# Three linked empty GpSimd instructions behind each of 512 indirect transfers

## The chip, the cores and the metric

The kernel runs on one core of one Trainium2 chip. The metric is the device time of one execution in microseconds (us); of the kernel before, the median of three runs is 880.05 us.

## The reference

An input x of 32 x 256 rows of 128 numbers (float32) goes through three layers that each add to it: half of a feed-forward layer with 16 experts, an attention-like layer with a complex running sum, and half of the same expert layer again. Cut to what matters:

```python
x = L0_attn_x
x = x + 0.5 * _L0_ffn_ref(_layernorm(x, axis=-1), ...)
x = x + _L0_attn_ref(_layernorm(x, axis=-1), ...)
x = x + 0.5 * _L0_ffn_ref(_layernorm(x, axis=-1), ...)

def _L0_ffn_ref(x, Wr, br, W1, b1, W2, b2):      # every row goes to its best two of 16 experts
    probs = softmax(xt @ Wr + br)
    w, idx = top_k(probs, 2)
    comb = zeros((T, E)).at[arange(T)[:, None], idx].add(w / sum(w))
    h = gelu(einsum('td,edh->teh', xt, W1) + b1)
    o = einsum('teh,eho->teo', h, W2) + b2
    return xt + einsum('teo,te->to', o, comb)

def _L0_attn_ref(x, gamma, wq, wk, wv, wa, wg, wo):
    q, k, v, a, g = xn @ wq, xn @ wk, xn @ wv, xn @ wa, xn @ wg
    # a becomes a complex factor of magnitude below one
    y_t = a_t * y_(t-1) + k_t * v_t               # an associative scan over the sequence
    return (q * real(y) * silu(g)) @ wo
```

## The kernel before

The 8192 rows are cut into four groups (g = 0 to 3) of 16 tiles of 128 rows. Each of the two expert layers (f = 0 and 1) handles a group as follows. The router (stages R and K) finds for each row its two experts and the place that it gets in a table sorted by expert, and leaves the places in `IDX`. GpSimd **scatters** (stage P) each tile twice, once for each chosen expert, into a table `rows_in` in the chip's memory: 32 indirect transfers for a group, the first 16 at L466 and the others at L474, with a small copy (L471) of the weights ahead of each eight of the latter. SyncE then loads `rows_in` in pieces into `xs` (L366) and the weights of the experts into `WUP` (L360). TensorE, with ScalarE, works through 24 **pairs** of tiles in a group (stage E, cut into sub-stages such as pairs 0 to 8, 8 to 20 and 20 to 24): it turns `xs` over (L776), multiplies with the first weights (L786) and, behind the gelu of ScalarE, with the second (L803). ScalarE moves each pair's result into `eo` (L540) and stores it into `rows_out`. GpSimd **gathers** (stage G) from there into `got` at L487, again 32 indirect transfers for a group, and VectorE adds `got` to `X` (stage C, L1069 and L1070). Between the layers a group goes through the attention stages (T, A0, A, I, H, A1, J, AP, U, A2, A3); its products on TensorE are at L863.

A table `ORDER` at the head of the file lists all stages; each engine walks it and takes its own part, so it sets the order on every engine. GpSimd's order is P00, P01, G00, P02, G01, P03, G02, P10, G03, P11, G10, P12, G11, P13, G12, G13 (the digits are f and g; G(0,3), G(1,1), G(0,2), P(1,3) and G(1,3) are issued in parts). There are 8 x 32 scatters and 8 x 32 gathers, 512 transfers.

GpSimd does not run ahead freely. Two tables, `PAIRS_BY` and `PRODUCTS_BY`, hold for each transfer how many pairs (semaphore `eo_sb`) and attention products (`proj_ps`) must be done before it is issued; `keep_behind` (L448) turns them into waits. A gather also waits for the stores of its group's pairs, a scatter for `IDX`. SyncE waits for the landed scatters of a group ahead of its first `xs` (L380, L381).

`link` (L419) lets an instruction raise a semaphore `pool_chain` at its end and makes the next instruction of GpSimd wait for it. 

Of the kernel before, what the change touches and what calls it, by code (L numbers as in the profile page):

```python
# [16 lines left out]
P = 128  # L17
# [3 lines left out]
G = 4  # L21
T = B * N // G // P
# [97 lines left out]

SLOT = {(f, g, 0): g for f in range(2) for g in range(G)}
SLOT.update({(f, g, 1): (g + 1) % G for f, g in HALVED})
# [3 lines left out]
def build(nc, x, gamma, wq, wk, wv, wa, wg, wo, wr, br, w1, b1, w2, b2, out):  # L126
# [43 lines left out]
    def rows_put(f, g, half):  # L170

        if half == 1:
            return XBUF + HALVED.index((f, g)), 16 * TILES[f, g, 1]
        rn = kind_no[("R", f, g)]
        return rn % XBUF, 16 * sum(TILES[st[1], st[2], 0] for st in kind_no if st[0] == "R"
                                       and kind_no[st] <= rn and kind_no[st] % XBUF == rn % XBUF)

    with ExitStack() as ctx:
# [236 lines left out]
        @block.gpsimd  # L415
        def _(pool):
            chain = [0]

            def link(ins):  # L419
                chain[0] += 1  # L420
                ins.then_inc(pool_chain, 1)
                pool.wait_ge(pool_chain, chain[0])

            pool.memset(zeros, 0.0).then_inc(zero_ready, 1)
            pool.memset(ones[:], 1.0)
            pool.memset(onesf[:], 1.0)
            link(pool.memset(ones_sq, 1.0))
            pool.affine_select(out=ident[:], in_=ones_sq, compare_op=ALU.is_equal, fill=0.0, base=0,
                               pattern=[[-1, P]], channel_multiplier=1)
            pool.affine_select(out=before[:], in_=ones_sq, compare_op=ALU.is_gt, fill=0.0, base=0,  # L430
                               pattern=[[1, P]], channel_multiplier=-1)
            link(pool.iota(iota_i, [[1, NT]], base=0, channel_multiplier=0))
            pool.tensor_scalar(centre[:], ident[:], 2.0, -2.0 / D, mult, add)
            link(pool.memset(keep[:], 1.0))
            pool.memset(keep[:, :, 0:1], 0.0)
            pool.memset(marks[:], 0.0)
            pool.tensor_copy(iota_f[:], iota_i).then_inc(consts, 1)
            pool.memset(B2[:], 0.0).then_inc(bias_clear, 1)

            pool.wait_ge(up_bias_in, 16)  # L440
            link(pool.tensor_copy(bias_parts[:, 0, :], raw_bias))
            link(pool.tensor_tensor(bias_rest, raw_bias, bias_parts[:, 0, :], sub))
            link(pool.tensor_copy(bias_parts[:, 1, :], bias_rest))
            pool.tensor_tensor(bias_parts[:, 2, :], bias_rest, bias_parts[:, 1, :], sub).then_inc(up_bias_split, 1)

            waited = [0, 0]

            def keep_behind(st, i):  # L448
                if i % 1 == 0 and PAIRS_BY[st][i // 1] > waited[0]:
                    waited[0] = PAIRS_BY[st][i // 1]  # L450
                    pool.wait_ge(eo_sb, waited[0])
                if i % 1 == 0 and PRODUCTS_BY[st][i // 1] > waited[1]:
                    waited[1] = PRODUCTS_BY[st][i // 1]
                    pool.wait_ge(proj_ps, waited[1])

            def scatter(n, m, f, g, half):
                slot, tiles = SLOT[f, g, half], TILES[f, g, half]
                b, (which, _) = kind_no[("R", f, g)] % XBUF, rows_put(f, g, half)
                first = T - tiles if half else 0
                parts = [range(first, first + tiles // 2), range(first + tiles // 2, first + tiles)]  # L460
                pool.wait_ge(rows_ready, n + 1)
                pool.wait_ge(zeroed[slot], 16 * ZEROS)
                for i, part in enumerate(parts):
                    for j in part:
                        keep_behind(("P", f, g, half), j - first)
                        pool.indirect_dma_start(rows_in[slot], bass.IndirectOffsetOnAxis(IDX[:, g, j, 0:1], 0),  # L466
                                                XL[:, b, j, :], None).then_inc(first_put[i], 16)
                for i, part in enumerate(parts):
                    pool.wait_ge(first_put[i], 8 * sum(TILES[st[1:]] for st in kind_no if st[0] == "P" and kind_no[st] <= m))
                    mine = slice(part[0], part[-1] + 1)  # L470
                    link(pool.tensor_copy(XL[:, b, mine, D:D + 1], WGT[:, g, 1, mine].unsqueeze(2)))  # L471
                    for j in part:
                        keep_behind(("P", f, g, half), tiles + j - first)
                        pool.indirect_dma_start(rows_in[slot], bass.IndirectOffsetOnAxis(IDX[:, g, j, 1:2], 0),  # L474
                                                XL[:, b, j, :], None).then_inc(scattered[which], 16)

            def gather(n, f, g, lo, hi):
                half = lo * T // 4 // TILES[f, g, 0]
                rows = (2 * TILES[f, g, half] + E - 1) * P
                for u in range(2):  # L480
                    pool.wait_ge(eo_out[u], 16 * (pairs_by[f, g, half] // SLOTS))
                for j in range(lo * T // 4, hi * T // 4):
                    if n > 0 and j % 4 == 0:
                        pool.wait_ge(combined, (n - 1) * 4 + j // 4 + 1)
                    for k in range(2):
                        keep_behind(("G", f, g, lo, hi), 2 * j - lo * T // 2 + k)
                        pool.indirect_dma_start(got[:, k, j, :], None, rows_out[SLOT[f, g, half]][0:rows, :],  # L487
                                                bass.IndirectOffsetOnAxis(IDX[:, g, j, k:k + 1], 0)).then_inc(got_in[j // 4], 16)

            for st in ORDER:  # L490
                if st[0] == "P":
                    scatter(kind_no[("K",) + st[1:]], kind_no[st], *st[1:])
                if st[0] == "G":
                    gather(gathers.index(st[1:3]), *st[1:])
# [696 lines left out]
```

## Time and profile before

| | |
|---|---|
| median of three runs | 880.05 us (880.0 to 881.23) |
| profiled execution, first to last instruction | 994.3 us |
| mean granted TensorE clock in it | 0.858 |
| TensorE busy in it | 725.1 us (73%) |
| VectorE, ScalarE busy | 546.3 us, 514.7 us |
| GpSimd busy | 590.6 us (59%), 551 instructions |
| indirect gathers, L487 | 256, mean 1117 ns |
| indirect scatters, L466 and L474 | 128 each, mean 1227 and 1065 ns |

The profiled execution's own time is known by its span alone, and that is 114.3 us longer than the median of the runs without a profile. So a time read from the profile is not simply a time of a timed run. In the page, a group's busy time is the number of instructions by their mean duration; the idle time behind it is that of its engine just before these instructions, by what ended it. "issue" means that nothing the profile shows was waited for.

### The profile page before, as it was taken

To read this page: it belongs to the slowest core of one execution; us is meant where nothing else is said; L and a number is where in the kernel's file an instruction comes from. 1 tells how busy PE (TensorE), PEld (TensorE's weight loads), DVE (VectorE), ACT (ScalarE), POOL (GpSimd) and SP (SyncE) were. 2 spreads that over 40 slices of the span, in tenths; PEclk is the share of its full clock that TensorE was granted. 3 is DMA by queue.
4 is the path that set the end of the run, shared out by engine and by line. 5 is a ranking of instruction groups with operands and counts; after the bars stand their busy time and mean duration, and the time that the engine had idled before them with its cause. 6 is when DMAs were issued, how large, how long until landed. Compare 5 with 4: busy or idle time off the path is not lost.

```text
span 994.3 us, 15862 instructions
## 1 busy us (share of the span) xinstructions
PE 725.1 (73%) x4409; PEld 607.2 (61%) x4410; DVE 546.3 (55%) x1352; ACT 514.7 (52%) x1071; POOL 590.6 (59%) x551
## 2 busy tenths in 40 slices
PE   4775888786876888669777967685968648977761
PEld 4234788685366873469644867534958627777650
DVE  7983103106689955799745996647876455010201
ACT  1111556455777637676277773576664315444340
POOL 2277441555777747758467457378657545655555
PEclk9995899889977989789788779795989759999986
DMA  9995587774146833176441456321758517778863
GB/s 327 299 348 165 149 234 228 208 202 130 40 123 195 224 111 105 42 202 194 121 124 46 129 161 202 99 66 40 217 167 250 141 41 199 221 207 226 234 201 103
DMA packets 188846, 167.13 MB, mean 168 GB/s; under 512 B 18976, under 2 KB 176480, under 8 KB 187744
## 3 DMA queue, kind: packets, MB, share of 16 engines
q1 hardware_dynamic: 120736, 106.83, 36.6%
q0 software_dynamic: 16384, 33.72, 11.5%
q10 hardware_dynamic: 51648, 25.63, 8.8%
q8 instruction: 39, 0.64, 0.3%
q14 instruction: 39, 0.32, 0.1%
HBM read 104.57 MB, written 61.51 MB: 167 GB/s over the span
## 4 chain that ended last, share of the span: by engine, by line
PE 48%; issue 12%; ACT 12%; another core or an unknown queue 9%; SPq 7%; DVE 5%; DMA 5%; ACTq 0%; DVEq 0%
PE bank L786 17%; PE bank L803 16%; PE bank L863 7%; DMA WUP<-up_weights 4%; PE bank L776 4%; ACT eo L540 2%; SPq L319 2%; PE bank L758 2%; SPq L360 1%; SPq L330 1%; ACT hidT L532 1%; PE bank L702 1%; ACT ci L623 1%; ACT xsT L551 1%
## 5 line engine op out<-in xcount | busy, mean ns | idle before, releaser
L487 POOL DMA_INDIRECT got<-rows_out,IDX x256 | 285.8, 1117 | 194.2 <-ACT eo L540 86.5
L786 PE MATMUL bank<-xsT,WUP 128*128 128x128 f32 x1564 | 240.0, 303 | 77.4 <-ACT xsT L551 51.1
L786 PEld LDWEIGHTS bank<-xsT,WUP 128*128 128x128 f32 x1564 | 218.8, 216 | 85.9 <-issue 75.2
L803 PE MATMUL bank<-W,hidT 128*128 x1564 | 221.0, 286 | 41.5 <-ACT hidT L532 32.1
L803 PEld LDWEIGHTS bank<-W,hidT 128*128 128x128 f32 x1564 | 199.3, 199 | 51.4 <-issue 49.6
L466 POOL DMA_INDIRECT rows_in<-XL,IDX x128 | 157.1, 1227 | 109.3 <-DVE IDX L1039 46.5
L474 POOL DMA_INDIRECT rows_in<-XL,IDX x128 | 136.3, 1065 | 91.7 <-ACT eo L540 53.7
L540 ACT ACTIVATE eo<-bank,xs 128x128 f32<-128x128 f32 x391 | 122.7, 367 | 109.9 <-PE bank L803 74.6
L532 ACT ACTIVATE hidT<-bank 128x512 f32<-128x512 f32 x200 | 118.1, 591 | 116.1 <-PE bank L786 72.8
L551 ACT ACTIVATE xsT<-bank 128x256 f32<-128x256 f32 x200 | 74.0, 377 | 86.2 <-remote 39.2
L863 PE MATMUL bank<-XT,WA 128*128 128x512 f32 x192 | 94.6, 654 | 21.2 <-DVE qg L1090 10.4
L776 PE MATMUL bank<-ident,xs 128*128 128x128 f32 x391 | 81.8, 301 | 5.7 <-issue 3.1
L1069 DVE TENSOR_TENSOR X<-got,X 128x512 f32<-128x512 f32 x32 | 22.0, 686 | 116.3 <-DMA got<-rows_out,IDX 102.2
L863 PEld LDWEIGHTS bank<-XT,WA 128*128 128x128 f32 x192 | 39.1, 207 | 72.8 <-issue 57.6
L1062 DVE TENSOR_TENSOR X<-bank,X 128x512 f32<-128x512 f32 x32 | 21.3, 687 | 96.5 <-issue 41.4
L776 PEld LDWEIGHTS bank<-ident,xs 128*128 128x128 f32 x391 | 56.4, 161 | 8.5 <-issue 8.2
L712 PE MATMUL bank<-WR,hidT 128*128 128x16 f32 x192 | 38.9, 341 | 21.9 <-issue 20.9
L712 PEld LDWEIGHTS bank<-WR,hidT 128*128 128x128 f32 x192 | 38.5, 297 | 23.9 <-issue 23.8
L758 PE MATMUL bank<-B,CT 128*128 128x512 f32 x64 | 37.0, 708 | 15.8 <-issue 9.0
L913 DVE BATCH_NORM_STATS2 stats<-X 128x6 f32<-128x128 f32 x192 | 38.3, 278 | 6.0 <-DMA X<-in_L_attn_x 5.8
L1011 DVE TENSOR_SCALAR den<-gexp 128x16 f32<-128x16 f32 x8 | 1.4, 173 | 62.0 <-ACT gexp L516 60.8
L969 DVE TENSOR_SCALAR XL<-X,rs,nb 128x128 f32<-128x128 f32 x128 | 33.8, 360 | 1.0 <-DVE rs L951 0.8
(150 smaller groups left out, 900.4 us busy)
## 6 DMA issues: line engine op xcount, KB each, us to landing
WUP<-up_weights SPq DMA_DIRECT2D x400, 128.0 KB
xs<-rows_in SPq DMA_DIRECT2D x100, 258.0 KB
rows_out<-eo ACTq DMA_DIRECT2D x91, 256.0 KB
rows_in<-kv SPq DMA_DIRECT2D x16, 774.0 KB, 12.1
X<-in_L_attn_x SPq DMA_DIRECT2D x4, 1024.0 KB, 7.7
rows_in<-XL,IDX POOLq DMA_INDIRECT x256
got<-rows_out,IDX POOLq DMA_INDIRECT x256
out<-X SPq DMA_DIRECT2D x4, 1024.0 KB
```

Source lines behind the costliest of these rows:

```text
L466: pool.indirect_dma_start(rows_in[slot], bass.IndirectOffsetOnAxis(IDX[:, g, j, 0:1], 0), XL[:, b, j, :], None).then_inc(first_put[i], 16)
L474: pool.indirect_dma_start(rows_in[slot], bass.IndirectOffsetOnAxis(IDX[:, g, j, 1:2], 0), XL[:, b, j, :], None).then_inc(scattered[which], 16)
L487: pool.indirect_dma_start(got[:, k, j, :], None, rows_out[SLOT[f, g, half]][0:rows, :], bass.IndirectOffsetOnAxis(IDX[:, g, j, k:k + 1], 0 ...
L532: act.activation(hidT[:, v, 0:tiles * 2 * P], ps[2 + v][:, 0:tiles * 2 * P], ACT.Gelu).then_inc(hid_sb, 1)
L540: ins = act.activation(eo[:, u // 2, t, :], ps[6 + u % 2][:, a * D:(a + 1) * D], ACT.Copy, scale=xs[:, buf, t, D:D + 1])
L551: act.activation(xsT[:, v, 0:tiles * P], ps[v][:, 0:tiles * P], ACT.Copy).then_inc(xsT_sb, 1)
L712: ins = pe.matmul(ps[4][:, j * E:(j + 1) * E], rowsT[i - 1][:, j % 4 * P:(j % 4 + 1) * P], WR[:], start=True, stop=True)
L758: pe.matmul(ps[5 - i][:], CT[:, half * P:(half + 1) * P], B2[:, i, :], start=True, stop=True).then_inc(bias_ps, 1)
L776: ins = pe.transpose(ps[u % 2][:, a * P:(a + 1) * P], xs[:, buf, u % 2 * 2 + a, 0:D], ident[:])
L786: ins = pe.matmul(ps[2 + u % 2][:, k * P:(k + 1) * P], WUP[:, u, a, c * P:(c + 1) * P], xsT[:, u % 2, a * P:(a + 1) * P], start=True, stop ...
L803: ins = pe.matmul(o, hidT[:, v, (2 * a + c) * P:(2 * a + c + 1) * P], W2[:, ds(e * H + c * D, D)], start=(c == 0), stop=(c == 1))
L863: pe.matmul(ps[turns_of[k % 6]][:], WA[:, w, :], XT[:, blk * 512:(blk + 1) * 512], start=True, stop=True).then_inc(proj_ps, 1)
```

## The change

Behind each of the 512 indirect transfers GpSimd issues three empty instructions, each linked: the second waits for the first, the third for the second, and whatever comes next on GpSimd (the next transfer, or the copy of the weights) for the third. The table `APART` is 1 for all of them. Nothing else is changed.

```diff
+APART = {
+            ('P', 0, 0, 0): (1, 1, 1, ...),
...
+            def keep_apart(st, i):
+                if APART[st][i]:
+                    link(pool.engine_nop())
+                    link(pool.engine_nop())
+                    link(pool.engine_nop())
+
@@ scatter, first half
                         pool.indirect_dma_start(rows_in[slot], bass.IndirectOffsetOnAxis(IDX[:, g, j, 0:1], 0),
                                                 XL[:, b, j, :], None).then_inc(first_put[i], 16)
+                        keep_apart(("P", f, g, half), j - first)
@@ scatter, second half
                         pool.indirect_dma_start(rows_in[slot], bass.IndirectOffsetOnAxis(IDX[:, g, j, 1:2], 0),
                                                 XL[:, b, j, :], None).then_inc(scattered[which], 16)
+                        keep_apart(("P", f, g, half), tiles + j - first)
@@ gather
                         pool.indirect_dma_start(got[:, k, j, :], None, rows_out[SLOT[f, g, half]][0:rows, :],
                                                 bass.IndirectOffsetOnAxis(IDX[:, g, j, k:k + 1], 0)).then_inc(got_in[j // 4], 16)
+                        keep_apart(("G", f, g, lo, hi), 2 * j - lo * T // 2 + k)
```

On GpSimd, at the first scatters of the program and the copy between them, there stood before:

```order
L466 DMA rows_in<-XL,IDX 6144x129 x15
L471 COPY XL<-WGT 128x8 [waits first_put0]
L474 DMA rows_in<-XL,IDX 6144x129 [waits pool_chain]
L474 DMA rows_in<-XL,IDX 6144x129 x7
```

There stands now, at the end of the sixteen first scatters (an "ISA" row is an empty instruction; lines 484 to 486 are those of `keep_apart`):

```order
L485 ISA [waits pool_chain]
L486 ISA [waits pool_chain]
L504 COPY XL<-WGT 128x8 [waits first_put0,pool_chain]
L507 DMA rows_in<-XL,IDX 6144x129 [waits pool_chain]
L484 ISA
L485 ISA [waits pool_chain]
L486 ISA [waits pool_chain]
L507 DMA rows_in<-XL,IDX 6144x129 [waits pool_chain]
```

No transfer changed its place among the others; between any two of them now stand three rows, and each transfer has a wait for the last of these.

## Rows read from the trace of the kernel before

**Rows 1.** The page: busy time of the engines.
```profile
PE 725.1 (73%) x4409; PEld 607.2 (61%) x4410; DVE 546.3 (55%) x1352; ACT 514.7 (52%) x1071; POOL 590.6 (59%) x551
```

**Rows 2.** GpSimd's waits: waited for, us in total, times, longest us.
```profile
POOL got L487 <- ACT eo L540: 86.5, 36, 12.6
POOL got L487 <- issue: 71.0, 207, 3.7
POOL rows_in L474 <- ACT eo L540: 53.7, 20, 9.8
POOL rows_in L466 <- DVE IDX L1039: 46.5, 3, 33.5
POOL rows_in L466 <- issue: 34.7, 113, 0.5
POOL rows_in L474 <- issue: 29.4, 94, 1.0
POOL rows_in L466 <- ACT eo L540: 28.1, 12, 7.8
POOL got L487 <- DMA rows_out<-eo: 22.2, 1, 22.2
```

**Rows 3.** Timeline of GpSimd: start us, us, engine, line [idle before <-releaser].
```profile
0.32 0.10 POOL L1182 MEMSET const-float32-0.0<- 128x1 f32 x1 [0.32 <-issue]
0.35 0.10 POOL L1182 MEMSET const-float32-1.0<- 128x1 f32 x1
...
7.28 0.39 POOL L443 CAST got<-got 16x256 bf16<-16x256 f32 x1
7.75 0.66 POOL L444 TENSOR_TENSOR got<-got 16x256 bf16<-16x256 f32 x1
...
62.51 0.96 POOL L466 DMA_INDIRECT rows_in<-XL,IDX  x1 [0.30 <-issue]
63.77 0.96 POOL L466 DMA_INDIRECT rows_in<-XL,IDX  x1 [0.30 <-issue]
64.74 0.23 POOL L471 COPY XL<-WGT 128x8 f32<-128x8 f32 x1
65.25 1.05 POOL L474 DMA_INDIRECT rows_in<-XL,IDX  x1 [0.28 <-POOL XL L471]
```

**Rows 4.** The page: busy, mean ns | idle before, of the three transfer groups.
```profile
L487 POOL DMA_INDIRECT got<-rows_out,IDX x256 | 285.8, 1117 | 194.2 <-ACT eo L540 86.5
L466 POOL DMA_INDIRECT rows_in<-XL,IDX x128 | 157.1, 1227 | 109.3 <-DVE IDX L1039 46.5
L474 POOL DMA_INDIRECT rows_in<-XL,IDX x128 | 136.3, 1065 | 91.7 <-ACT eo L540 53.7
```

**Rows 5.** The chain that ended last, near 90 us: start us, us, what.
```profile
83.10 6.26 issue
89.36 3.08 DMA xs<-rows_in
```

**Rows 6.** Timeline of GpSimd, later places.
```profile
41.95 1.62 POOL L466 DMA_INDIRECT rows_in<-XL,IDX  x1 [33.55 <-DVE IDX L1039]
...
232.95 0.95 POOL L466 DMA_INDIRECT rows_in<-XL,IDX  x1 [1.78 <-ACT eo L540]
...
249.99 0.98 POOL L474 DMA_INDIRECT rows_in<-XL,IDX  x1 [2.97 <-PE bank L863]
...
272.53 0.96 POOL L474 DMA_INDIRECT rows_in<-XL,IDX  x1 [0.31 <-issue]
...
296.69 1.23 POOL L487 DMA_INDIRECT got<-rows_out,IDX  x1 [2.22 <-ACT eo L540]
...
330.37 0.99 POOL L487 DMA_INDIRECT got<-rows_out,IDX  x1 [1.35 <-ACT eo L540]
...
411.46 2.01 POOL L487 DMA_INDIRECT got<-rows_out,IDX  x1 [0.30 <-issue]
...
977.28 0.94 POOL L487 DMA_INDIRECT got<-rows_out,IDX  x1 [0.87 <-issue]
...
986.08 0.94 POOL L487 DMA_INDIRECT got<-rows_out,IDX  x1 [0.30 <-issue]
```

**Rows 7.** Timeline of VectorE.
```profile
342.65 0.68 DVE L1069 TENSOR_TENSOR X<-got,X 128x512 f32<-128x512 f32 x1
...
410.37 2.29 DVE L1095 SCALAR_TENSOR_TENSOR S<-S 128x2048 f32<-128x2048 f32 x1
...
988.58 0.69 DVE L1069 TENSOR_TENSOR X<-got,X 128x512 f32<-128x512 f32 x1 [9.14 <-DMA got<-rows_out,IDX]
```

**Rows 8.** Timeline of SyncE: the load of `xs` at 274.91 us.
```profile
274.91 1.49 SPq L366 DMA_DIRECT2D xs<-rows_in  x3
```

**Rows 9.** TensorE's waits: us in total, times, longest us.
```profile
PE bank L786 <- DMA WUP<-up_weights: 15.1, 11, 2.7
PEld bank L786 <- DMA WUP<-up_weights: 10.2, 8, 2.2
```

**Rows 10.** The chain that ended last, 270 to 292 us: start us, us, what.
```profile
288.24 1.80 ACT S L619
290.04 0.28 ACT xsT L551
290.32 0.14 issue
290.45 1.62 PE bank L786 x6
```

24 rows, old and new, of the table APART are left out of this document.

## The prediction

> **What bounds the kernel now.** I read the busy times first: TensorE leads with 73% of the span, GpSimd has 59%, and none is full [rows 1]. So the ends of stages decide, and I went to GpSimd's waits, the only engine that the change touches. The waits for pairs, for `IDX` and for stores are real cover: GpSimd stood still by order of the two tables or for a true dependence [rows 2]. The "issue" entries are no cover: the timeline shows that a gap of 0.30 us stands between any two transfers even when nothing is waited for, so that a transfer costs 0.96 + 0.30 = 1.26 us [rows 3]. Then come the places where somebody waits for GpSimd: the first `xs` at 89.36 us, and the last gathers [rows 5 to 7].
>
> GpSimd's load between its first transfer at 41.95 us and the end of its last at 986.08 + 0.94 = 987.02 us [rows 6], a stretch of 945 us: the transfers take 285.8 + 157.1 + 136.3 = 579 us [rows 4], the 18 small copies about 4 us (0.23 us each, [rows 3]), and 512 gaps of 0.30 us make 154 us. That is 737 us. The other 208 us are cover.
>
> **The price of the three empty instructions.** The trace has none of them, so I bound it. From above: a linked copy. From the end of the transfer at 64.73 us to the start of the next at 65.25 us there are 0.52 us, against 0.30 us without the copy [rows 3]; the gap behind the copy is still 0.28 us. So one linked instruction of 0.23 us costs 0.22 us, and three cost 0.66 us. From below: unlinked small memsets start 0.03 us apart [rows 3], three are 0.09 us; and less than nothing isn't excluded for the program as a whole, since spaced transfers may disturb others less (a rival below). Between: a linked follower starts 0.08 us behind the end of its predecessor (7.28 + 0.39 = 7.67, next at 7.75, [rows 3]), and an empty instruction should take less than the 0.10 us of the smallest memset and more than the 0.03 us between two starts; with 0.06 us each the three cost 3 x 0.06 + 2 x 0.08 = 0.34 us. I take 0.33 us, nearest to the linked rows. The load grows by 512 x 0.33 = 169 us.
>
> The small memset of 0.10 us [rows 3] says how long GpSimd's own overhead is here. The Trainium skill (GPSIMD Engine Reference, section 2.1, Instruction dispatch) gives "tens of cycles" for a call, which agrees with that row; the same page (section 3.1) lists about 156 ns of dispatch for a VectorE instruction and says that GpSimd has one more software hop. By that larger figure three would cost 0.47 us, and the load would grow by 240 us; no run here shows it yet.
>
> Something comes back. Transfers that fall beside a long VectorE instruction are stretched: 2.01 us at 411.46 us beside a 2.29 us instruction [rows 6, 7], against 0.94. Over all, the means 1117, 1227 and 1065 ns [rows 4] against 0.94 to 0.96 us make 256 x 0.17 + 128 x 0.27 + 128 x 0.11 = 92 us of stretch. With 0.33 us of 1.59 us in empty instructions, at most 92 x 0.33 / 1.59 = 19 us of it can fall on these instead of adding to them; I count half, 10 us.
>
> **The sum in the profiled execution.** (a) Start. The first group's 32 scatters run without any wait between them, and SyncE has its weights requested by 83.10 us and sits until 89.36 us for the last of them [rows 5]. Nothing covers these: 32 x 0.33 = +10.6 us, and everything after moves with it. (b) Middle. The waits between swallow the price again and again, but not everywhere. The third group's second scatters restart after a wait of 2.97 us at 249.99 us [rows 6]; the 11 transfers since the wait at 232.95 us bring 3.6 us, so about 1 us is left; the 16 behind bring 5.3, and the last, at 272.53 us, is some 6 us late. It gates the `xs` at 274.91 us [rows 8], which is used only once ScalarE has got through its attention work at 290.04 us [rows 10]; with 3.08 us for the load [rows 5] some 10 us are free, and it costs nothing. The 32 gathers behind it add 10.6 us less what five waits hold beyond their gap, some 5 us (the first at 296.69 us, 2.22 us long, the last at 330.37 us, 1.35 us): 12 us late at 330.37 us [rows 6], where VectorE takes the data at 342.65 us [rows 7], 11 us after: +1 us. Later stages have the waits on GpSimd of rows 2, up to 12.6 us at a time, and the scatters that gate them lie further ahead of their use. (c) End. The last eight gathers follow a wait at 977.28 us, which the store of the last pair ends; they run back to back to 986.08 us and VectorE takes the last of them at 988.58 us [rows 6, 7]. Seven intervals and the six transfers ahead, less their waits: +3 us. Sum: 10.6 + 1 + 3 = +15 us, 994.3 to 1009 us.
>
> **From there to the timed runs.** The runs are 114 us shorter than this execution, and what is shorter in them no row tells. If GpSimd's 737 us stay as they are and the other engines are quicker, the cover is 208 - 114 = 94 us, and 169 us don't fit. If all shrink alike, the +15 us stand. I take the middle: half of the 114 us (57) out of the cover, which shortens the stretch to 888 us. The load is then 737 + 169 - 10 = 896 us, and one wait can't go: the 22.2 us for the first group's stores [rows 2], since these pairs start only behind the first scatters. That makes 918 us against 888 us: +30 us. The forecast is 880 + 30 = 910 us. The cover is then used up nearly everywhere, so GpSimd would be the bound of most stages.
>
> **The rivals.**
> - GpSimd is the full bound. All 114 us come out of the cover: 896 + 22 against 945 - 114 = 831 us is +87 us, 967 us. For it: GpSimd has few instructions, and its transfers are steady at 0.94 to 0.96 us, as if nothing disturbed them. Against it: the stretches from VectorE's instructions would shrink with these.
> - The cover holds. +15 us as summed for the profiled execution, or a price near 0.2 us: 895 us. For it: the many waits of rows 2. Against it: the missing 114 us.
> - Faster. The transfers come in bursts 1.26 us apart, and TensorE waited 15.1 + 10.2 us for weights that SyncE loads beside them [rows 9]. With 1.59 us between them the scatters and gathers take a fifth less of the DMA engines while they run. Should most of these 25 us go, and the price be near its lower bound (0.09 us: start 3 us, end 1 us), the program gains up to 20 - 4 = 16 us: 864 us, likelier about 872 us. It decides where the price is under about 0.2 us. The Trainium skill (DMA: Bandwidth & Descriptors, section SWDGE vs HWDGE vs iDMA) says that a DMA engine takes turns between the queues of the two kinds, which is the mechanism of this rival; the trace shows only the waits.
> - The edit doesn't do what it says. The three are dropped or are handled beside the transfer's own 0.30 us gap: 880 us. Against it: the linked copy was not hidden in that gap [rows 3].
>
> **How the numbers follow.** Forecast 910 us (its own range 895 to 935): 0.38. Full bound, 967 us: 0.24. Cover holds, 895 us: 0.21. Faster, 872 us: 0.11. No effect: 0.06. The range that leaves 2 in 10 out starts at 885 us, short of the last two cases, and ends at 985 us, beyond the full bound, for a price of more than 0.33 us; at 0.66 us and no cover it would be far beyond. A measurement of this kernel tells about 0.2% from no change. Slower by more than that: 0.38 + 0.24 + 0.21 = 0.83; faster 0.11; within 0.06.
>
> **What would show it.** The price: the distance of the starts of two transfers that wait for nothing, 1.26 us before; 1.59 us expected. Step (a): the first `xs` at 100 us instead of 89.36 us. Step (c): the last gather 11 us after the final wait instead of 8.8 us. The cover: GpSimd's waits for `eo` (168 us by rows 2) fall to under 60 us. The middle: the profiled span grows less than the timed median. I am wrong if the distance is under 1.4 us, if it is over 1.8 us, or if the first `xs` doesn't move.

## The result and the profile after

The changed kernel takes 986.25 us (median of 4 runs, 984.53 to 990.76) against 880.02 us before: the ratio is 1.121, 95% interval 1.1177 to 1.1243. It is slower by 106 us. The forecast was 910 us with a range of 885 to 985 us; the measured median is just above the range, and nearest to the rival of the full bound (967 us).

The profiled execution of the changed kernel spans 985.1 us and took 986.86 us, so here profile and timed runs are one thing. The one of before in the rows ahead of the prediction spans 994.3 us, and no timed run of that kernel came near it. Profiled once more ("before again" below), the unchanged kernel spans 884.9 us in a run of 886.66 us. So the differences below are taken against this second profile. Why the first one was 110 us longer is not settled.

GpSimd in the changed kernel (start us, us, engine, line [idle before <-releaser]; "POOLq L486" is the third empty instruction). First come rows near 90 us, where the tables hold no transfer back; the third of these rows is the next group's first scatter, which also waits for that group's `IDX`. Then come rows near 185 us, and the end:

```profile
90.55 0.96 POOL L507 DMA_INDIRECT rows_in<-XL,IDX  x1 [0.44 <-POOLq L486]
91.95 1.11 POOL L507 DMA_INDIRECT rows_in<-XL,IDX  x1 [0.44 <-POOLq L486]
93.95 0.96 POOL L498 DMA_INDIRECT rows_in<-XL,IDX  x1 [0.89 <-POOLq L486]
95.35 0.96 POOL L498 DMA_INDIRECT rows_in<-XL,IDX  x1 [0.44 <-POOLq L486]
...
181.72 0.94 POOL L521 DMA_INDIRECT got<-rows_out,IDX  x1 [0.86 <-POOLq L486]
183.09 0.94 POOL L521 DMA_INDIRECT got<-rows_out,IDX  x1 [0.43 <-POOLq L486]
184.89 0.94 POOL L521 DMA_INDIRECT got<-rows_out,IDX  x1 [0.85 <-ACT eo L575]
186.27 0.94 POOL L521 DMA_INDIRECT got<-rows_out,IDX  x1 [0.44 <-POOLq L486]
...
967.01 0.94 POOL L521 DMA_INDIRECT got<-rows_out,IDX  x1 [1.25 <-issue]
968.38 1.15 POOL L521 DMA_INDIRECT got<-rows_out,IDX  x1 [0.43 <-POOLq L486]
...
976.86 0.94 POOL L521 DMA_INDIRECT got<-rows_out,IDX  x1 [0.44 <-POOLq L486]
```

Where there were gaps of 0.30 us [rows 3], there are two kinds now: 0.44 us, and 0.86 us. Of the 512 transfers, 238 wait for the third empty instruction alone; the other 274 have a further wait, 253 of them one of the two tables. Of a transfer's several waits only one hangs on the transfer itself. The others stand ahead of it as an instruction of their own, a **stand-alone wait**, here between the third empty and the transfer. The traces bear this out: the changed kernel's has 17667 instructions and that of before 15862, which is the 1536 empties and 269 more. 234 transfers have 0.4 to 0.5 us of idle time ahead of them and 257 have 0.8 to 1.0 us. The row at 184.89 us shows why this is easily misread: it names pairs (`eo`) as the releaser, but its gap is the same 0.85 us as at places where none were waited for.

Who waits for GpSimd (columns: us in total, times, longest), first before again, then the changed kernel; SyncE's queue for the scattered rows, VectorE for the gathered ones:

```profile
SPq L366 <- DMA rows_in<-XL,IDX: 109.6, 7, 40.8
DVE X L1069 <- DMA got<-rows_out,IDX: 93.6, 10, 20.7
```

```profile
SPq L392 <- DMA rows_in<-XL,IDX: 287.7, 7, 65.2
DVE X L1104 <- DMA got<-rows_out,IDX: 181.6, 17, 41.5
```

And TensorE ahead of the first instruction that needs `xs` (busy, mean ns | idle before), again before and after:

```profile
L776 PE MATMUL bank<-ident,xs 128*128 128x128 f32 x391 | 80.4, 296 | 10.2 <-DMA xs<-rows_in 8.5 <-issue 1.5
```

```profile
L811 PE MATMUL bank<-ident,xs 128*128 128x128 f32 x391 | 81.3, 299 | 69.3 <-DMA xs<-rows_in 66.9 <-issue 1.9
```

TensorE's idle time for scattered rows went from 8.5 to 66.9 us, while its own instructions last as long as before. 47.3 of the 66.9 us stand at two places, the first loads of the third and of the fourth group of the second expert layer:

```profile
770.58 1.09 PE L811 MATMUL bank<-ident,xs 128*128 128x128 f32 x4 [31.50 <-DMA xs<-rows_in]
...
863.16 1.09 PE L811 MATMUL bank<-ident,xs 128*128 128x128 f32 x4 [15.79 <-DMA xs<-rows_in]
```

GpSimd's own waits tell the rest. Before again, then the changed kernel:

```profile
POOL got L487 <- ACT eo L540: 28.2, 24, 8.7
POOL got L487 <- DMA rows_out<-eo: 23.0, 1, 23.0
POOL rows_in L474 <- ACT eo L540: 13.7, 17, 2.0
POOL got L487 <- PE bank L863: 11.4, 16, 3.3
POOL rows_in L466 <- ACT eo L540: 6.4, 9, 3.6
```

```profile
POOL got L521 <- POOLq L486: 147.7, 229, 1.0
POOL rows_in L498 <- POOLq L486: 71.7, 112, 1.0
POOL rows_in L507 <- POOLq L486: 63.6, 94, 0.9
POOL got L521 <- ACT eo L575: 19.3, 22, 1.2
POOL got L521 <- DMA rows_out<-eo: 15.5, 3, 13.6
```

No wait for `eo` is longer than 1.2 us in the changed kernel, so the tables hardly hold GpSimd back any more. From its first transfer to its last it stands in waits of over 1 us for 33.7 of 935.9 us: it is the bound of nearly the whole stretch.

An account of this stretch, from the first transfer to the end of the last, worked out from GpSimd's timelines:

| us | before again | changed | difference |
|---|---|---|---|
| stretch | 835.6 | 935.9 | +100.3 |
| busy (transfers and copies) | 594.8 | 568.4 | -26.4 |
| gaps up to 1 us | 157.0 | 333.7 | +176.7 |
| gaps over 1 us (true waits) | 83.8 (23) | 33.7 (14) | -50.1 |

The load grew by 176.7 - 26.4 = 150 us, 50 us of cover took a third of it, and 100 us came out as time. The other 6 us to the 106 are that this profiled run of before was itself some 6 us above its median.

The trace of the changed kernel also holds the instructions that the views leave out, and they show where a stand-alone wait comes in. Around the transfer at 181.72 us the one before it ends at 180.86 us, and the three empties start at 180.86, 180.95 and 181.01 us. The stand-alone wait takes 17 ns at 181.00 us, which is when the second empty has just run and the third has not, and the transfer starts 0.72 us behind it. It is so throughout. Each of the 255 gaps of 0.78 to 0.95 us has a stand-alone wait in it, 249 of them 0.14 us behind the end of the previous transfer, and in 232 the transfer starts 0.715 to 0.745 us after the wait. None of the 223 gaps of 0.28 to 0.5 us has one. So 0.86 us is 0.14 us until the wait is passed and 0.72 us from there to the transfer.

### The profile page after: what moved, and what is told of

The parts are those of the page before. It is cut to its first block and busy times, and to the rows that moved or that the text cites. A ratio compares the mean times of both kernels' runs of the same rounds, so it can differ in the third digit from the quotient of the medians.

```text
span 985.1 us, 17667 instructions
## 1 busy us (share of the span) xinstructions
PE 707.6 (72%) x4409; PEld 590.0 (60%) x4410; DVE 546.8 (56%) x1352; ACT 522.1 (53%) x1071; POOL 575.6 (58%) x551
## 5 line engine op out<-in xcount | busy, mean ns | idle before, releaser
L521 POOL DMA_INDIRECT got<-rows_out,IDX x256 | 289.2, 1130 | 185.1 <-POOLq L486 147.7
L821 PE MATMUL bank<-xsT,WUP 128*128 128x128 f32 x1564 | 229.2, 293 | 48.5 <-ACT xsT L586 37.5
L821 PEld LDWEIGHTS bank<-xsT,WUP 128*128 128x128 f32 x1564 | 207.9, 207 | 57.2 <-issue 43.7
L838 PE MATMUL bank<-W,hidT 128*128 x1564 | 213.2, 279 | 3.4 <-ACT hidT L567 1.6
L498 POOL DMA_INDIRECT rows_in<-XL,IDX x128 | 134.2, 1048 | 118.4 <-POOLq L486 71.7
L838 PEld LDWEIGHTS bank<-W,hidT 128*128 128x128 f32 x1564 | 192.3, 193 | 9.4 <-issue 6.4
L507 POOL DMA_INDIRECT rows_in<-XL,IDX x128 | 140.9, 1101 | 93.3 <-POOLq L486 63.6
L811 PE MATMUL bank<-ident,xs 128*128 128x128 f32 x391 | 81.3, 299 | 69.3 <-DMA xs<-rows_in 66.9
L811 PEld LDWEIGHTS bank<-ident,xs 128*128 128x128 f32 x391 | 53.8, 157 | 74.9 <-issue 74.4
L910 PE MATMUL bank<-WO,kv 128*128 128x128 f32 x128 | 28.9, 405 | 16.9 <-DVE kv L1168 16.2
L910 PEld LDWEIGHTS bank<-WO,kv 128*128 128x128 f32 x128 | 28.3, 311 | 17.6 <-issue 16.7
```

What stands on the lines that cost most here:

```text
L811: ins = pe.transpose(ps[u % 2][:, a * P:(a + 1) * P], xs[:, buf, u % 2 * 2 + a, 0:D], ident[:])
L821: ins = pe.matmul(ps[2 + u % 2][:, k * P:(k + 1) * P], WUP[:, u, a, c * P:(c + 1) * P], xsT[:, u % 2, a * P:(a + 1) * P], start=True, stop ...
L838: ins = pe.matmul(o, hidT[:, v, (2 * a + c) * P:(2 * a + c + 1) * P], W2[:, ds(e * H + c * D, D)], start=(c == 0), stop=(c == 1))
L910: ins = pe.matmul(ps[4 + i][:, j * D:(j + 1) * D], by_time(kv[:])[:, 4 * i + j, :], WO[:], start=True, stop=True)
```

## Experiments

All ratios are against runs of the kernel before on the same chip, with their 95% interval.

**Before again.** The unchanged kernel.

> The kernel before, unchanged, profiled once more. Its first profile spans 994 us where its timed runs take 880 us, while the changed kernel's profile spans 985 us and its timed runs take 986 us. Theory A (that one profiled execution was not like the timed ones): the span comes out near 880 us now, with the same GpSimd load of about 737 us and so much less waiting on GpSimd. Theory B (recording slows this kernel and not the changed one): the span is near 994 us again while the time stays at 880 us.

Measured: 880.37 us (ratio 0.9977, 0.994 to 1.0015), span 884.9 us. GpSimd was busy for 594.8 us and its waits over 1 us were 83.8 us, not the 213 us of the first profile. Theory A holds: the first profile of before was one odd execution. All timed runs of before in this study lie between 875.5 and 890.2 us.

**The tables' wait on the first empty.** The empties stand ahead of each transfer, at all three places where `keep_apart` is called; the first is shown.

```diff
                         keep_behind(("P", f, g, half), j - first)
+                        keep_apart(("P", f, g, half), j - first)
                         pool.indirect_dma_start(rows_in[slot], ...).then_inc(first_put[i], 16)
-                        keep_apart(("P", f, g, half), j - first)
```

> The same three linked empty instructions for every transfer, but ahead of it, so that the table's wait hangs on the first empty instruction and the transfer waits for the third alone. Theory 1 (three linked empties cost 0.14 us, and a transfer that has a second wait beside the one for the third costs 0.42 us more): every gap is 0.44 us, GpSimd's load grows by 512 x 0.14 = 72 us only, which fits into the cover of the timed runs (208 - 114 = 94 us), and the time is 885 to 910 us. Rival 2 (the empties cost 0.14 us or 0.56 us by themselves, wherever they stand): as slow as the changed kernel, 986 us.

Measured: 906.57 us (1.0259, 1.0193 to 1.0325). The timeline of GpSimd at the place shown above for the changed kernel:

```profile
179.00 0.94 POOL L522 DMA_INDIRECT got<-rows_out,IDX  x1 [0.44 <-POOLq L486]
180.38 0.95 POOL L522 DMA_INDIRECT got<-rows_out,IDX  x1 [0.43 <-POOLq L486]
181.76 0.95 POOL L522 DMA_INDIRECT got<-rows_out,IDX  x1 [0.43 <-POOLq L486]
```

The gaps are 0.43 to 0.49 us now (500 of 512) except for true waits, with as many empties as in the changed kernel. The further wait hangs on the first empty: the trace has 17398 instructions, none of the 269 beyond the empties. 80 of the 106 us are gone. So most of the loss is neither the empties nor the pacing, but where the further wait stands.

**A second wait alone, no empties.**

```diff
             def keep_behind(st, i):
+                old = list(waited)
...
+                if old != waited:
+                    pool.wait_ge(pool_chain, chain[0])
```

> No empty instructions. Each transfer that has a wait of the tables gets a second wait, for a chain value that was reached long before. If any second wait costs 0.42 us, the gaps ahead of some 230 transfers rise from 0.30 to 0.72 us, the load grows by about 97 us and the time is 890 to 920 us. If a second wait costs only where it is released late, that is just before the transfer, the gaps stay at 0.30 us and the time at 880 us.

Measured: 881.15 us (0.9994, 0.9962 to 1.0026). The trace has 234 instructions more than that of before, and these stand-alone waits cost nothing here:

```profile
179.45 0.94 POOL L490 DMA_INDIRECT got<-rows_out,IDX  x1 [0.31 <-issue]
180.70 0.95 POOL L490 DMA_INDIRECT got<-rows_out,IDX  x1 [0.30 <-issue]
181.95 0.95 POOL L490 DMA_INDIRECT got<-rows_out,IDX  x1 [0.30 <-issue]
```

**Three empties, unlinked.** `link(pool.engine_nop())` becomes `pool.engine_nop()`, three times.

> The three empty instructions behind each transfer, not linked: no semaphore, no wait. Theory 1: the price is in the links and in the second wait; the gap grows by under 0.1 us, the load by under 50 us, which the cover takes: 880 to 890 us. Rival 2 (an empty instruction holds GpSimd by itself): gaps of 0.44 and 0.86 us as in the changed kernel and 986 us.

Measured: 882.9 us (1.0015, 0.9987 to 1.0042), gaps 0.30 us. The 1536 empties are free as long as nothing waits for them.

**One linked empty.** Two of the three lines in `keep_apart` are removed.

> One linked empty instruction behind each transfer instead of three, at the same place. If the price is mostly in the empties and their links, it falls to a third: gaps of about 0.35 us and, where the tables' wait stands as a wait of its own between the empty and the transfer, 0.49 us; the load grows by under 50 us and the time is 885 to 895 us. If it is mostly the stand-alone wait (0.42 us at 274 transfers, 115 us) which can't be passed early once a linked instruction stands ahead, the gaps there stay at about 0.77 us and the time is 930 to 955 us.

Measured: 883.5 us (1.0007, 0.9983 to 1.0031). Both expectations were too high. The 274 stand-alone waits are still there, between the empty and the transfer (the trace has the 512 empties and the same 269 instructions more than that of before), and the gaps are 0.31 us with and without them:

```profile
96.48 0.96 POOL L496 DMA_INDIRECT rows_in<-XL,IDX  x1 [0.31 <-POOLq L484]
...
182.76 0.95 POOL L519 DMA_INDIRECT got<-rows_out,IDX  x1 [0.30 <-ACT eo L573]
```

**A met wait ahead of every transfer**, on the kernel with the tables' wait on the first empty.

```diff
                     link(pool.engine_nop())
+                    pool.wait_ge(zero_ready, 1)
```

> As the run with the empties ahead of the transfer and the tables' wait on the first of them (906.6 us, gaps of 0.44 us), and now a wait that was met long ago stands as an instruction of its own between the third empty and every transfer. Theory 1 (such a wait costs 0.42 us at this place even when it is met): all gaps 0.86 us, the load is 750 + 72 + 215 = 1037 us and the time 42 + 1037 + some 35 = 1100 to 1130 us. Rival (in the changed kernel these 0.42 us were real waiting for pairs, not a price of the wait): gaps 0.44 us, 907 us.

Measured: 1075.39 us (1.219, 1.2144 to 1.2235). The semaphore was met before the first transfer, so nothing is really waited for, and yet:

```profile
179.84 0.94 POOL L523 DMA_INDIRECT got<-rows_out,IDX  x1 [0.85 <-POOLq L486]
181.64 0.94 POOL L523 DMA_INDIRECT got<-rows_out,IDX  x1 [0.85 <-ACT eo L576]
183.44 0.94 POOL L523 DMA_INDIRECT got<-rows_out,IDX  x1 [0.85 <-POOLq L486]
```

Nearly every gap (491 of 512) is 0.85 to 0.92 us. This makes the 0.42 us a price of the place and not a wait for pairs. The time is 25 us below the range expected: the gaps came as foretold, but the transfers were stretched less, so that the load is 990 us and not 1037 us.

**The met wait ahead of the first empty** instead.

```diff
                 if APART[st][i]:
+                    pool.wait_ge(zero_ready, 1)
+                    pool.wait_ge(consts, 1)
                     link(pool.engine_nop())
```

> The same stand-alone wait, met long ago, but ahead of the first empty, right behind the previous transfer. Theory 1 (GpSimd's sequencer gets through it while the previous transfer is still generated, so only a place behind a linked instruction costs): gaps 0.44 us, 907 us. Rival (a stand-alone wait costs 0.42 us wherever it stands among linked empties): gaps 0.86 us, 1100 us.

Measured: 907.16 us (1.0271, 1.0234 to 1.0308), gaps 0.44 us: the same as without these waits. (Two are added so that one must stand alone.)

```profile
178.41 0.94 POOL L524 DMA_INDIRECT got<-rows_out,IDX  x1 [0.43 <-POOLq L488]
179.79 0.94 POOL L524 DMA_INDIRECT got<-rows_out,IDX  x1 [0.44 <-POOLq L488]
```

The same instruction, three places earlier, costs nothing. The trace shows why: in 477 of 480 such gaps a stand-alone wait is passed inside the gap, mostly 0.23 us ahead of the transfer's start. Ahead of the transfer at 178.41 us that is at 178.19 us, when all three empties ahead of this transfer have run. This transfer's own stand-alone wait stands ahead of those empties, so the one passed at 178.19 us is the next, which stands behind the transfer in the program: GpSimd passes it before the transfer itself starts.

**Linked empties only where no table's wait is.**

```diff
-                if APART[st][i]:
+                if APART[st][i] and not held[0]:
```

`held` is set where the tables bring a wait for this transfer; the empties stand ahead of the transfer.

> Three linked empties only ahead of the transfers that have no wait of the tables (259), none ahead of the others. Load theory: 259 x 0.14 = 36 us more load, which the cover of some 90 us takes except at the start and the end: 883 to 892 us. If every spaced transfer cost 0.36 us on the mean wherever it stands, the load would grow by 93 us and the time would be 910 us.

Measured: 896.43 us (1.0144, 1.0108 to 1.018). It lies between the two expectations, 4 us above the range of the load theory; the gaps are 0.30 and 0.44 us as expected. Of the 36 us some 14 came out as time, where that theory had 3 to 12: the cover took the larger part, but less than expected.

**Two linked empties.** One of the three lines in `keep_apart` is removed.

> Two linked empties behind each transfer. One gave gaps of 0.31 us everywhere, three 0.44 and, at the 274 transfers with a stand-alone wait, 0.86 us. Theory S (the stand-alone wait and the transfer's own preparation are run through ahead of time as long as at most one instruction ahead of them still has to wait for a link): with two linked empties only the second waits for a link, so the stand-alone wait is still passed early, gaps are 0.37 us or less everywhere, the load grows by at most 36 us and the time is 885 to 900 us. Rival L (any link that is still open ahead of the stand-alone wait brings the 0.42 us): gaps of 0.37 and about 0.79 us, 512 x 0.07 + 274 x 0.42 = 151 us more load and 950 to 975 us.

Measured: 959.79 us (1.0874, 1.0814 to 1.0935). GpSimd's timeline:

```profile
95.64 0.96 POOL L497 DMA_INDIRECT rows_in<-XL,IDX  x1 [0.38 <-POOLq L485]
...
181.07 0.94 POOL L520 DMA_INDIRECT got<-rows_out,IDX  x1 [0.37 <-POOLq L485]
182.80 1.06 POOL L520 DMA_INDIRECT got<-rows_out,IDX  x1 [0.79 <-POOLq L485]
```

Rival L holds to 0.01 us in both gaps. The step from one to two linked empties is the one that brings the 0.42 us: with two, the second has to wait for the first, and the stand-alone wait comes behind an instruction that is itself still waiting. In this trace too all 274 gaps of 0.78 to 0.95 us have a stand-alone wait in them, mostly 0.07 us behind the end of the previous transfer, with the transfer 0.715 to 0.745 us behind it (237 of 274).

**Three empties, the last alone linked.**

```diff
-                    link(pool.engine_nop())
-                    link(pool.engine_nop())
+                    pool.engine_nop()
+                    pool.engine_nop()
                     link(pool.engine_nop())
```

> Three empties behind each transfer of which only the last is linked (the transfer behind waits for it; the second and third wait for nothing). If the price comes from the links between the empties, it is gone as with one linked empty: gaps of 0.31 to 0.35 us and 880 to 890 us. If it comes from three instructions between the transfers together with a wait on the last, gaps are 0.44 and 0.86 us and the time is 986 us.

Measured: 891.51 us (1.0127, 1.006 to 1.0194), slightly above the range expected, gaps 0.34 to 0.36 us with and without the stand-alone wait:

```profile
97.62 0.96 POOL L498 DMA_INDIRECT rows_in<-XL,IDX  x1 [0.35 <-POOLq L486]
...
183.36 0.94 POOL L521 DMA_INDIRECT got<-rows_out,IDX  x1 [0.34 <-POOLq L486]
```

The number of empties, the wait of the transfer for the last, and the 274 stand-alone waits are those of the changed kernel; only the two inner links are gone, and with them 95 of the 106 us.

**The changed kernel without the tables' waits**, and **the kernel before without them.** `keep_behind` returns at once.

> The changed kernel without the waits of the two tables (the waits for IDX, stores and combined data stay), so that hardly any transfer has a stand-alone wait. Load theory: gaps of 0.44 us, the load is about 820 us, and the time is 895 to 925 us: most of the changed kernel's loss goes though its empties all stay. Rival (the loss comes from the spacing by the empties, not from the waits beside them): still 986 us.

> The kernel before without the tables' waits, as the yardstick of the run above. The tables hold GpSimd back behind TensorE's pairs; in the undisturbed profile of before they cost it about 50 us of waiting. If that waiting is only cover, 875 to 885 us; if holding the transfers back keeps the queues free for the weights, 885 to 905 us.

Measured: 914.25 us (1.0361, 1.0305 to 1.0417) and 880.95 us (1.0005, 0.997 to 1.0041). With all linked empties in place the loss is 33 us instead of 106. In the kernel before the tables' waits change nothing that can be measured: without them GpSimd stands in 6 waits of over 1 us for 89.2 us, against 83.8 us in 23 before again. They were cover and nothing else.

Set by what each version adds to GpSimd's gaps, counted as transfers by the measured gap less 0.30 us:

| version | added, us | time, us |
|---|---|---|
| before; one linked empty | 0; 5 | 880; 883.5 |
| last alone linked | 512 x 0.05 = 26 | 891.5 |
| linked only where free | 259 x 0.14 = 36 | 896.4 |
| tables' wait on the first empty | 512 x 0.14 = 72 | 906.6 |
| three linked, no tables' waits | 72 + 37 x 0.42 = 88 | 914.3 |
| two linked | 512 x 0.07 + 274 x 0.42 = 151 | 959.8 |
| changed kernel | 72 + 274 x 0.42 = 187 | 986.3 |
| met wait ahead of every transfer | 512 x 0.56 = 287 | 1075.4 |

(37 transfers have waits other than those of the tables.) The timelines agree: GpSimd's gaps of up to 1 us sum to 157 us in before again, and in the versions of the table, from one linked empty down, to 4, 23, 32, 65, 83, 148, 177 and 270 us more. The order of the times is that of the added load, without exception, whether it comes from empties or from waits. The first 72 us cost 25 us against the kernel before on the same chip, about a third; from 88 to 151 us 45 of 63; from 187 to 287 us 89 of 100. That is how cover is used up: none of the versions shows an edge, and part of every small load is paid at the start and the end, where there is no cover.

None of the versions is faster than the kernel before.

## Why the prediction was wrong

**The price and the load: right in sum by luck, wrong inside.** The bounds of 0.09 and 0.66 us held, and 0.33 us on the mean stands against (512 x 0.14 + 274 x 0.42) / 512 = 0.365 us. But the term was thought of as one price for every transfer, from the 0.08 us between linked followers and 0.06 us for an empty. A linked empty adds only 0.07 us (0.31, 0.37, 0.44 us for one, two, three), and the first is hidden in the 0.30 us gap. By that alone the price is 0.14 us, and the load would have grown by 72 us and not by 169 us. The larger part, 115 of 187 us, came from something that the prediction did not have: a further wait, in 253 of 274 cases that of the tables, which hung on the transfer itself before and cost nothing there, had to stand alone once the link's wait took its place. It was to be seen in the code, where `keep_behind` sets its wait right behind the one of `link`, and the row of the copy at L504, with `first_put0` and `pool_chain`, shows such a pair. That two errors met near the measured mean is luck. Where nothing stretches the first of two transfers, their starts are 1.38 to 1.40 us or 1.80 to 1.83 us apart and not the 1.59 us expected; the signs of being wrong, under 1.4 and over 1.8 us, have both come, by some 0.02 us.

**The stretched transfers: larger, and the cause not shown.** 10 us were counted, at most 19; busy time fell by 26.4 us (594.8 to 568.4). That it fell because empties took the place of the stretch, as the prediction has it, no run shows: with the gaps 0.14 us wider it is 594.1 and 595.8 us (the tables' wait on the first empty, without and with the met waits), so nothing came back, and the kernel before itself had 582.9 us in its first profile. It is clearly lower only in the three slowest versions (574.0, 568.4 and 562.6 us). The net load, 159 us forecast, is 150 us by the account above.

**The cover: the step that failed.** The prediction took 208 us of cover from the profile of before and then, because the timed runs were 114 us shorter, took off half of the difference, 57 us, "the middle". The second profile of before has 83.8 us over 1 us and 751.8 us of load in its stretch; so all of the difference was cover, and GpSimd's load was as large in the timed runs as in the odd profile. The rival of the full bound had this right: 94 us of cover and 967 us. It still fell 19 us short: 33.7 us of waits stayed where it kept 22 us, and the load in the changed kernel is 902 us where it had 896 us. So 57 of the 76 us by which the forecast missed lie in this one step. The chances had the full bound at 0.24 only, though the one fact that bore on it, that every undisturbed transfer took the same 0.94 to 0.96 us, spoke for it.

**Start and end: the mechanism right, the size off.** The first `xs` was expected 10.6 us later. The first stage has no waits of the tables, so it pays 0.14 us for each transfer, 32 x 0.14 = 4.5 us. SyncE's first load starts 5.7 us later; here before again, then the changed kernel:

```profile
88.68 1.49 SPq L366 DMA_DIRECT2D xs<-rows_in  x3
```

```profile
94.42 1.59 SPq L392 DMA_DIRECT2D xs<-rows_in  x3
```

At the end the last gather starts 9.9 us after the final wait (967.01 to 976.86 us) against 8.8 us [rows 6], 7 x 0.14 = 1 us and a stretched transfer; 11 us was expected.

**The middle: refuted.** The +1 us, and the free 10 us ahead of the third group's `xs`, were read off the odd profile; TensorE's idle time for `xs` grew by 58 us. 6.5 us of it stand at the third group (275.05 us). The most, 31.5 and 15.8 us, stand in the last two groups of the second layer, for which the prediction said that the scatters lie further ahead of their use.

**Two signs that say nothing.** GpSimd's waits for `eo` were to fall to under 60 us; they are 38 us in the changed kernel, but 48 us before again too. And the profiled span did grow less than the median, it even fell from 994.3 to 985.1 us, but only because the first profile was the odd one.

**Faster: refuted here.** TensorE's waits for weights are 15.1 + 13.1 us in before again and 10.0 + 10.6 us in the changed kernel, so something may have been given back, as that rival said, but under 8 us against 150 us of load. Its condition, a price near the lower bound, is met by the run with one linked empty, and that isn't faster either. **No effect** is refuted too, though it is what three unlinked empties do.

A page of the Trainium skill bears on the place of the wait (Perfetto Trace Analysis, section Per-instruction lifecycle, under DMA Instruction — SWDGE): the sequencer pushes an instruction with its semaphore wait into a wait queue and goes on to fetch and decode the next. The traces agree as far as they go: with the met wait ahead of the first empty, GpSimd passes it while the transfer ahead of it has not begun, and in the changed kernel it passes an instruction behind the third empty while that empty is still held. They also show where this ends: in the changed kernel the stand-alone wait is passed no earlier than 0.14 us behind the previous transfer, once the second empty has run, and the transfer starts 0.72 us later. Where the wait is passed earlier, these 0.72 us lie beside the previous transfer's 0.94 us and cost nothing. What GpSimd does in the 0.72 us, and why it passes a wait behind one linked empty early but not behind two, isn't shown.

## What to carry to other kernels

On an engine with many short instructions, look for every place where a new wait pushes an old one off the instruction that carried it: an old wait that was free can become an instruction of its own, and what it costs depends on whether something still held stands ahead of it. Put the waits on the first instruction of a linked chain, or leave out the inner links. And where a profile's span isn't that of the timed runs, take another profile before the sum is made: here GpSimd's load carried over within 20 us of 750, and 130 us of its waits did not.

## What the runs showed of the hardware

Empty instructions that nothing waits for are free on GpSimd between indirect transfers (1536 of them: 1.0015, 0.9987 to 1.0042). A stand-alone wait costs nothing behind a transfer (0.9994, 0.9962 to 1.0026) or behind one linked empty (gaps of 0.31 us), and 0.42 us behind two or three linked ones, in the latter case even for a semaphore met long before (906.6 to 1075.4 us for all 512 transfers). Behind two or three linked empties the transfer starts 0.715 to 0.745 us after the stand-alone wait is passed (469 of 529 such gaps). The gap of 0.30 us between two indirect transfers hides one linked empty whole. The busy time of the same 512 transfers and copies isn't fixed: 562.6 to 595.8 us over the versions, and 582.9 and 594.8 us in two executions of one kernel.
